# Context keys and values of the cross attention made right behind the last expert tile

## The reference

```python
x = x + _L0_attn_ref(_layernorm(x), W_q, W_kv, W_o)          # layer 0, attention in Fourier space
x = x + _L0_xattn_ref(_layernorm(x), k, skip, ctx, ctx, 8)   # layer 0, long convolution
x = x + _L0_ffn_ref(_layernorm(x), ...)                      # 8 experts, each token goes to 2
x = x + _L1_attn_ref(_layernorm(x), ...)                     # stage 4 of the kernel
x = x + _L1_xattn_ref(_layernorm(x), ctx, wq, bq, wkv, bkv, wp, bp)   # stage 5
x = x + _L1_ffn_ref(_layernorm(x), w_gate, w_up, w_down)     # stage 6
```

```python
q = _qdq(x) @ _qdq(wq).T + bq        # _qdq: rounded to 255 levels of the row's largest magnitude
kv = cond @ wkv.T + bkv              # cond is the context: nothing here depends on x
k, v = jnp.split(kv, 2, axis=-1)
attn = jax.nn.softmax(jnp.einsum('bnhd,bmhd->bhnm', q, k) * scale, axis=-1)
o = jnp.einsum('bhnm,bmhd->bnhd', attn, v).reshape(B, N, C)
out = _qdq(o) @ _qdq(wp).T + bp
```

## Time and profile before

| | |
|---|---|
| median of three runs | 777.13 us (776.04 to 778.58) |
| span of the profiled execution | 774.9 us |
| busy PE / DVE / ACT / POOL | 590.2 / 459.4 / 319.3 / 257.2 us |
| mean granted clock of PE | 0.887 of full speed |

### The profile page before, as it was taken

How to read it: one execution, slowest core, us unless ns; L and a number is a source line. 1 busy time by engine, 2 the same in 40 slices (tenths; PEclk the granted TensorE clock), 3 DMA queues, 4 the chain that set the end, 5 groups by cost and what they waited for, 6 DMA issues and landing times.

```text
span 774.9 us, 12670 instructions
## 1 busy us (share of the span) xinstructions
PE 590.2 (76%) x4241; PEld 425.4 (55%) x4242; DVE 459.4 (59%) x998; ACT 319.3 (41%) x747; POOL 257.2 (33%) x300
## 2 busy tenths in 40 slices
PE   3857896447499999999356989899889677763674
PEld 3446343434288888898223656576575265542332
DVE  3677999672544555455254453535365736767686
ACT  1511200423333333333254654717473535555454
POOL 4930687656000000000366863909423300000000
PEclk9969999555699999999878999999999889895698
DMA  7694202455401101110242000000001300000000
GB/s 273 222 369 154 87 0 66 152 173 207 156 29 54 54 27 54 54 55 19 62 129 65 1 0 2 1 1 0 1 1 47 117 1 3 2 2 1 0 27 27
DMA packets 34251, 52.17 MB, mean 67 GB/s; under 512 B 3097, under 2 KB 24161, under 8 KB 33825
## 3 DMA queue, kind: packets, MB, share of 16 engines
q1 hardware_dynamic: 31680, 43.49, 16.9%
q0 software_dynamic: 2528, 8.13, 2.9%
HBM read 40.60 MB, written 11.01 MB: 67 GB/s over the span
## 4 chain that ended last, share of the span: by engine, by line
PE 52%; DVE 16%; POOL 12%; ACT 11%; issue 4%; DMA 3%; another core or an unknown queue 0%; SPq 0%; ACTq 0%; DVEq 0%
PE bank L1536 16%; PE bank L1549 5%; PE bank L1685 4%; POOL sm L509 3%; POOL rq L502 3%; POOL qs L504 2%; POOL rq L500 2%; PE bank L1415 2%; ACT pT L805 2%; PE bank L1444 2%; PE bank L1446 2%; PE bank L1445 2%; DMA wraw<-in_L_ffn_W 1%; PE bank L1845 1%; PE bank L1946 1%
## 5 line engine op out<-in xcount | busy, mean ns | idle before, releaser
L659 ACT ACTIVATE hf<-bank,be 128x256 f32<-128x256 f32 x120 | 50.4, 471 | 79.4 <-PE bank L1536 73.1
L1536 PE MATMUL bank<-h,wsp 128*128 128x256 f16 x720 | 81.3, 273 | 2.2 <-DVE h L1090 1.5
L490 POOL DMA_INDIRECT yg<-expert_rows,pos x16 | 15.5, 970 | 192.5 <-DMA expert_rows<-yb 188.0
L1536 PEld LDWEIGHTS bank<-h,wsp 128*128 x720 | 69.6, 98 | 12.1 <-issue 3.9
L1088 DVE CAST h<-hf 128x512 f16<-128x512 f32 x60 | 25.6, 427 | 65.8 <-ACT hf L659 64.3
L704 ACT ACTIVATE sm<-sm,nm 128x128 f32<-128x128 f32 x128 | 49.8, 394 | 1.0 <-DVE nm L1201 1.0
L472 POOL TENSOR_TENSOR kvp<-xnT,cxT 128x512 f32<-128x512 f32 x32 | 35.7, 1137 | 42.3 <-ACT xnT L563 32.4
L569 ACT CAST wsp<-wraw 128x2048 f16<-128x2048 f32 x12 | 22.6, 1900 | 63.5 <-DMA wraw<-in_L_ffn_W 63.5
L449 POOL TENSOR_TENSOR wsp<-wraw,wsp 128x512 f16<-128x512 f32 x40 | 45.8, 1178 | 8.7 <-ACT wsp L569 8.4
L1198 DVE SCALAR_TENSOR_TENSOR sm<-bank,const 128x512 f32<-128x512 f32 x32 | 22.1, 691 | 38.5 <-PE bank L1652 38.5
L1536 PE MATMUL bank<-xgT,wsp 128*128 128x256 f16 x360 | 44.2, 282 | 0.1
(11 more groups left out here) (295 smaller groups left out, 1342.7 us busy)
## 6 DMA issues: line engine op xcount, KB each, us to landing
wraw<-in_L_ffn_W SPq DMA_DIRECT2D x16, 512.0 KB
wraw<-in_L_ffn_W SPq DMA_DIRECT2D x8, 1024.0 KB
sorted_rows<-early POOLq DMA_DIRECT2D x2, 1920.0 KB, 16.6
xg<-sorted_rows SPq DMA_DIRECT2D x15, 256.0 KB, 2.8
expert_rows<-yb SPq DMA_DIRECT2D x15, 256.0 KB, 2.2
cxT<-in_ctxT SPq DMA_DIRECT2D x2, 1024.0 KB, 9.1
tap<-in_taps SPq DMA_DIRECT2D x1, 2048.0 KB, 13.9
x<-in_x SPq DMA_DIRECT2D x1, 1024.0 KB, 5.9
```

The source lines that it names most:

```text
L659: last = nc.scalar.activation(hf[:, p, SLOTS * k:SLOTS * k + SLOTS], bank[2 * (layer - 1) + p][:, SLOTS * k:SLOTS * k + SLOTS], ACT.Gelu, ...
L1536: last = nc.tensor.matmul(b[:, SLOTS * (f % 2):SLOTS * (f % 2) + SLOTS], w[a_][:, c, P * f:P * f + P], inp[:, b_, c, :], start=(c == 0 and ...
```

## The change

The products of the context with `wkv` move from stage 5 to the end of the experts, and so does what belongs to them.

- **Inputs.** SP issues `wkvT`, `bv5` and `bk5` before its loop over the expert tiles, then waits for `wab_moved` and issues `cxT` (1 MB). ACT's copy of `wab` into `wqb` (1536 columns) stands for that after the first hidden layer of the first expert tile, no longer after the last tile.
- **Places.** `wkvT` lies beside `wqb` in the place of the raw expert weights; `kx2` and `vpad` lie over the split expert weights; `bv5` and `bk5` lie over `b3` and `wg`.
- **PE** makes the values (16 matmuls) and the keys (8 matmuls) right behind the last expert tile. The values use banks 6, 7, 0, 1 and the keys banks 2, 6, 7, 1, so the keys wait for DVE's reading of the values.
- **DVE** waits for the last expert product, then clears half of `vpad` (2048 elements a partition), sets the ones, makes `bkm` and adds the values' bias.
- **ACT** writes the keys, two products before and two after the first `deviation` of stage 4.
- **Stage 5.** `sdiag` is made on ACT, by 8 instructions of 128 columns, where POOL did it in one; POOL keeps only the clearing of `n4` and the sum with `bp5`, both behind `xi_ready`. The queries go to banks 6, 7, 4, 5. `queries_keys(0)` waits for two of the four `q5T` (semaphore `prep5_act` at 14) and no longer for all four query products; that wait stands in `keys_queries(0)`.

```diff
@@ SP
+            sp.dma_start(wkvT[:], ...).then_inc(sem("context5_loaded"), 16)
+            sp.dma_start(bv5[:], ...).then_inc(sem("context5_loaded"), 16)
+                sp.dma_start(bk5[:], ...).then_inc(sem("context5_loaded"), 16)
+            sp.wait_ge(sem("wab_moved"), 1)
+            sp.dma_start(cxT[:].rearrange("p c t s -> p (c t s)"), a["ctxT"]).then_inc(sem("cxT_loaded"), 16)
             with sp.Fori(0, ET // 2 - 1) as i:
...
@@ POOL
-            pool.wait_ge(sem("x4_added"), NT + 1)
-            nc.gpsimd.memset(vpad[:].rearrange("p t h d -> p (t h d)"), 0.0).then_inc(sem("prep5_pool"), 1)
+            pool.wait_ge(sem("w5_loaded"), 64)
+            pool.wait_ge(sem("xi_ready"), 1)
             nc.gpsimd.memset(n4[:].rearrange("p u n -> p (u n)"), 0.0).then_inc(sem("prep5_pool"), 1)
-            pool.wait_ge(sem("prep5_pool"), 1)
-            nc.gpsimd.memset(vpad[:, :, :, 16:17], 1.0).then_inc(sem("prep5_pool"), 1)
-            pool.wait_ge(sem("scale5_ready"), 1)
-            nc.gpsimd.tensor_tensor(sdiag[:], ..., ALU.mult).then_inc(sem("prep5_pool"), 1)
-            pool.wait_ge(sem("w5_loaded"), 112)
-            pool.wait_ge(sem("xi_ready"), 1)
             nc.gpsimd.tensor_tensor(x[:], x[:], bp5[:].unsqueeze(1).to_broadcast([P, NT, D]), ALU.add).then_inc(sem("prep5_pool"), 1)
@@ ACT
             hidden(1, 0, 0)
+            act.wait_ge(sem("w_split_dve"), 6)
+            nc.scalar.copy(wqb[:, :, 0]..., wab[:]...).then_inc(sem("wab_moved"), 1)
             with act.Fori(0, ET // 2) as i:
...
+            act.wait_ge(sem("bkm_ready"), 1)
+            keys5(0)
+            keys5(1)
             deviation(4, 0, 2)
+            keys5(2)
+            keys5(3)
             xnT_pair(0)
...
+            act.wait_ge(sem("scale5_ready"), 1)
+            for t in range(NT):
+                nc.scalar.activation(sdiag[:, t, :], cst["ident"], ACT.Copy, scale=xsc[:, 1, t:t + 1]).then_inc(sem("sdiag_ready"), 1)
@@ DVE
+            dve.wait_ge(sem("l3_psum"), ET)
+            then(nc.vector.memset(vpad[:, :, :, 16:32], 0.0))
+            nc.vector.memset(vpad[:, :, :, 16:17], 1.0)
+            dve.wait_ge(sem("context5_loaded"), 48)
+            nc.vector.tensor_tensor(bkm[:], ..., ALU.mult).then_inc(sem("bkm_ready"), 1)
+            for k in range(4):
+                dve.wait_ge(sem("prep5_psum"), k + 1)
+                nc.vector.tensor_tensor(vpad[:, 2 * k:2 * k + 2, :, 0:16], bank[VALUE_BANKS[k]]..., ALU.add).then_inc(sem("v5_ready"), 1)
@@ PE
+            pe.wait_ge(sem("context5_loaded"), 48)
+            pe.wait_ge(sem("cxT_loaded"), 32)
+            for k in range(4):
+                values_of(k)
             pe.wait_ge(sem("y_ready"), ET + CREDIT)
+            for k in range(4):
+                c, half = k // 2, k % 2
+                if k:
+                    pe.wait_ge(sem("v5_ready"), (1, 2, 4)[k - 1])
+                for ic in range(DC):
+                    last = nc.tensor.matmul(bank[KEY_BANKS[k]][:], wkvT[:, ic, P * c:P * c + P], ...)
+                last.then_inc(sem("prep5_psum"), 1)
...
             turn_pair(1)
+            pe.wait_ge(sem("prep5_act"), 8)
             queries_low(0, 0)
...
             def queries_keys(p):
                 pe.wait_ge(sem("prep5_act"), 14 if p < 4 else 16)
                 if p == 0:
-                    pe.wait_ge(sem("q5r_ready"), 4)
+                    pe.wait_ge(sem("prep5_act"), 12)
                     pe.wait_ge(sem("v5_ready"), 4)
...
             def keys_queries(p):
                 pe.wait_ge(sem("nT_ready"), p + 1)
+                if p == 0:
+                    pe.wait_ge(sem("q5r_ready"), 4)
```

More of the change, by code:

```diff
@@ L227, in decoder_kernel @@
         wqb = sb("wqb", [P, 3, 2, 8, 64], F32, sq4)
+        wkvT = sb("wkvT", [P, DC, 512], F32, sq4)
         sq4.close()
@@ L268, in decoder_kernel @@
         ewT = sb("ewT", [P, 2, DC, D], BF16, s5)
-        bkm = sb("bkm", [P, DC, 2], F32, s5)
-        kx2 = sb("kx2", [P, DC, NT, 2, P], F32, s5)
-        vpad = sb("vpad", [P, NT, H4, 32], F32, s5)
         sdiag = sb("sdiag", [P, NT, P], F32, s5)
@@ L669, in _ @@
             hidden(1, 0, 0)
+            act.wait_ge(sem("w_split_dve"), 6)
+            nc.scalar.copy(wqb[:, :, 0].rearrange("p c h n -> p c (h n)"), wab[:].rearrange("p c h n -> p c (h n)")).then_inc(sem("wab_moved"), 1)
             with act.Fori(0, ET // 2) as i:
@@ L676, in _ @@
             expert_out(ET // 2, 0)
-            act.wait_ge(sem("w_split_dve"), 6)
-            nc.scalar.copy(wqb[:, :, 0].rearrange("p c h n -> p c (h n)"), wab[:].rearrange("p c h n -> p c (h n)")).then_inc(sem("wab_moved"), 1)
             preload(ACT.Ln)
@@ L685, in xnT_pair, with keys5 @@
                                bank[3 + i][:].rearrange("p (c n) -> p c n", c=DC)).then_inc(sem("xnT_act"), 1)
+            def keys5(k):
+                c, half = k // 2, k % 2
+                act.wait_ge(sem("prep5_psum"), k + 5)
+                for par in range(2):
+                    nc.scalar.activation(kx2[:, c, 4 * half:4 * half + 4, par, :], bank[KEY_BANKS[k]][:].rearrange("p (t s) -> p t s", t=4), ACT.Identity,
+                                         bias=bkm[:, c, par:par + 1], scale=cst["parity"][:, par:par + 1]).then_inc(sem("prep5_act"), 1)
+            act.wait_ge(sem("bkm_ready"), 1)
+            keys5(0)
+            keys5(1)
             deviation(4, 0, 2)
+            keys5(2)
+            keys5(3)
             xnT_pair(0)
@@ L1251, in _ @@
                 dve.wait_ge(sem("prep5_act"), half + 11)
[L1252 to L1253 removed]
+                dve.wait_ge(sem("prep5_psum"), k + 13)
+                nc.vector.tensor_tensor(q5r[:, 2 * k:2 * k + 2, :].rearrange("p t s -> p (t s)"), bank[QUERY_BANKS[k]][:],
                                         sx5[:, 4 * half:4 * half + 4, :].rearrange("p t s -> p (t s)"), ALU.mult).then_inc(sem("q5r_ready"), 1)
[L1255 to L1259 removed]
             def most(p):
@@ L1576, in _, with values_of @@
                     turn_rows(i + 1, u)
-            pe.wait_ge(sem("y_ready"), ET + CREDIT)
+            def values_of(k):
+                for t in range(2 * k, 2 * k + 2):
+                    for ic in range(DC):
+                        last = nc.tensor.matmul(bank[VALUE_BANKS[k]][:, D * (t % 2):D * (t % 2) + D], cxT[:, ic, t, :], wkvT[:, ic, D:2 * D], start=(ic == 0), stop=(ic == DC - 1))
+                last.then_inc(sem("prep5_psum"), 1)
[3 more added lines that the diff above has]
+                values_of(k)
+            pe.wait_ge(sem("y_ready"), ET + CREDIT)
+            for k in range(4):
+                c, half = k // 2, k % 2
+                if k:
+                    pe.wait_ge(sem("v5_ready"), (1, 2, 4)[k - 1])
+                for ic in range(DC):
+                    last = nc.tensor.matmul(bank[KEY_BANKS[k]][:], wkvT[:, ic, P * c:P * c + P],
+                                            cxT[:, ic, 4 * half:4 * half + 4, :].rearrange("p t s -> p (t s)"), start=(ic == 0), stop=(ic == DC - 1))
+                last.then_inc(sem("prep5_psum"), 1)
             pe.wait_ge(sem("w4_loaded"), 48)
@@ L1759, in _ @@
             x_done(pe, 4, NT - 1)
-            pe.wait_ge(sem("w5_loaded"), 112)
-            pe.wait_ge(sem("cxT_loaded"), 32)
-            for c in range(DC):
-                for half in range(2):
-                    for ic in range(DC):
-                        last = nc.tensor.matmul(bank[2 * c + half][:], wkvT[:, ic, P * c:P * c + P],
-                                                cxT[:, ic, 4 * half:4 * half + 4, :].rearrange("p t s -> p (t s)"), start=(ic == 0), stop=(ic == DC - 1))
-                    last.then_inc(sem("prep5_psum"), 1)
+            pe.wait_ge(sem("w5_loaded"), 64)
             pe.wait_ge(sem("prep1_ready"), 6)
@@ L1776, in turn_x @@
                     last.then_inc(sem("xiT_psum"), 1)
-            def values_of(k):
-                for t in range(2 * k, 2 * k + 2):
-                    for ic in range(DC):
-                        last = nc.tensor.matmul(bank[(4, 5, 0, 1)[k]][:, D * (t % 2):D * (t % 2) + D], cxT[:, ic, t, :], wkvT[:, ic, D:2 * D], start=(ic == 0), stop=(ic == DC - 1))
-                last.then_inc(sem("prep5_psum"), 1)
             pe.wait_ge(sem("eqi_ready"), 1)
```

68 lines of the change are left out of this document (28 added, 40 removed).

## The result

| | kernel before | changed kernel |
|---|---|---|
| median of the timed runs, us | 777.33 (773.76 to 780.83, 6 runs) | 770.66 (762.68 to 772.0, 6 runs) |
| span of the profiled execution, us | 774.9 | 770.2 (772.0 in all) |

The ratio of the changed kernel's time to the time before is 0.9897, 95% interval 0.9864 to 0.993: about 8 us faster. The prediction was 767.1 us, with a range from 763.8 to 771.0. The median lies inside the range, 3.6 us above the value. A second series of the same kernel gave 766.59 us (764.9 to 770.25, 6 runs; ratio 0.9888, 0.9859 to 0.9918). The mean of all twelve runs is 768.0. Of the six runs of the version with halves, two (771.55 and 775.66 us, the profiled one) lie over 1.5% above its fastest; its ratio is made from the other four, whose median is 765.98.

The account below looks back on a forecast made before the run. Stage 5's preparation was bound by a DVE-PE chain holding 7.06 us of value matmuls, while PE waited 16.64 us after the experts. -2.4 - 7.9 + 0.3 = -10.0 us: span 764.9, median 767.1, range 763.8 to 771.0.

Parts of the forecast that it names:

- (a): Stage 5's preparation: without POOL's clearing of vpad, DVE's L906 falls from 2.29 to 0.17 us, -2.1 us.
- (b): Stage 5's preparation: without POOL's sdiag, DVE's eight L1235 blocks take 2.24 us and not 3.88, -1.6 us.
- rival C: Stage 5: the two long DVE lines are not POOL's doing, only the values' 7.9 us go: 769.5 us; chance 0.06.
- (c): Stage 5: sdiag costs ACT 2.6 us, its spreading ends 1.4 us after xi; (a) to (c) together -2.4 us.
- (d): Stage 5's preparation: the values leave and nothing of the 7.92 us comes back as a wait, -7.9 us.
- rival A: Stage 5's preparation: PE at full clock there, so L1805 and perhaps first scores run faster: -12.7, 764.4 us; chance 0.15.
- (e): Behind stage 5's first scores ACT is the next to be late, with 0.7 us left: not late.
- (f): Stage 5's first scores: L1827 now follows half-clock matmuls and may slow by 0 to +1.2 us; +0.3 taken.
- Start of the experts: ACT's copy of wab fits into idle time and the third tile's rows land in time: cost 0, at worst +1 us.
- End of the experts: Values and keys fit into PE's 16.64 us wait before the first turn: 0, with ends -0.5 and +2.5 us.
- rival B: Before stage 4, late keys or a falling clock give back +1 to +3.5 us: about 769.5 us; chance 0.22.
- D: Rival: without the values the loop stays at half clock in all seven later blocks, +22 us: 779; chance 0.03.

Follow-up runs that it names:

- the version with halves: Changed kernel, but PE spreads the first four sdiag blocks once ACT has made four, not all eight; median 767.7 us, ratio 0.9859.
- the version with filler: Changed kernel with sdiag spread in halves, plus nine unread 512-column products while PE waits for sdiag; median 765.52 us, ratio 0.986.
- With the values back: Changed kernel with value products and DVE's four additions again between query products and first scores, keys left early; median 777.06 us, ratio 1.0012.
- its version with fillers: Kernel before plus unread products in stage 4's first waits and stage 6's tiles; median 776.56 us, ratio 1.0001.
- warm everywhere: Halves and nine unread products in the preparation, plus unread products in stage 4's first waits and stage 6's tiles, against changed kernel; 762.52 us, ratio 0.9837.
- changed, warm in 4 and 6: Changed kernel plus unread products in stage 4's first waits and stage 6's tiles, none in stage 5's preparation; median 759.62 us, ratio 0.9803.

## Why the prediction was right, and where it was not

**(a), (b): right.** L906 was forecast at 0.17 and took 0.17; the eight blocks at 2.24 took 2.19. Both stalls return when POOL works (2.35 and 3.83 us), so rival C is out.

**(c): right in kind.** `sdiag` took ACT 2.44 us (2.6 forecast, from L840's row), the spreading 3.78 (3.52). It ended 16.2 us after the last sum of stage 4 (614.45 less 598.21), as forecast (612.2 less 595.95). `xi` was ready at 612.94, so the spreading is later by 1.5 us (1.4 forecast). What I did not see is that the turn behind it would run in part at half clock: 1.69 us, where it took 1.07 in the kernel before (as in the version with filler).

**(d): the sum right, by luck; the term for the queries wrong.** The chain of waits of the changed kernel:

```profile
617.43 0.70 DVE xn L1266
618.16 1.53 ACT xnT L795 x2
619.73 1.27 PE bank L1836 x16
```

The query products, which I left at 3.45 us (half clock), ran in 1.90 at full, as rival A had it. And "Nothing of the 7.92 us comes back as a wait" failed: PE waits 1.11 us for `xnT`. These two errors are one. Before, the second `q5T` was ready 3.4 us after the start of the query products (616.47 to 619.9), just as they ended. Now it is ready 3.0 us after it (616.7, with the first record missing from the trace, to 619.7), and in the kernel before's second profile, with full clock, 2.9. So the full clock ends the products 1.5 us sooner and the scores start only 0.4 sooner; the rest is the wait. The way from the end of the spreading to the query products, with the slower turn, took 2.2 and not 1.9 us. -1.5, +1.1 and +0.3 cancel: 21.52 us measured, 21.6 forecast. With the values back, the wait is hidden again, and the step measures 6.7, not 7.9. The forecast's 31.9 before came from a profile with its queries at half clock; against the one with full clock (30.20) the same change wins 8.7.

**(e): right.** ACT was free in time; L802 waited 1.06 us for PE (0.7 forecast).

**(f): the number right, its ground not.** The scores took 1.27 us in the chain, 1.24 before (+0.3 forecast). The products in front of them ran at full clock and not at half, so the case that I priced didn't come.

**Start of the experts: right, no cost.** ACT's copy of `wab` stood at 211.46 for 1.47 us, SP issued `cxT` at 212.96 and the third tile's rows at 213.69, and PE turned them at 222.74 without a wait (222.68 before).

**End of the experts: right to half a us** for every instruction that was placed. The last addition ended at 383.5 (383.6 forecast), the last key product at 389.65 (390.1), the first pair was turned at 392.3 (at most 393), `xnT_pair(0)` started at 393.06 (by 393.6). The remark on the gathers was not put to a test: DVE's memset ended at 378.13, the first gather came at 378.91.

**The clock in stage 4: mis-sized.** The 0 with an upper end of +2.5 "if the clock falls there" was too low. Seven profiles have both products at the end of the experts and no filler in stage 4. Two took 203.2 and 203.3 us, as before; five took 205.9 to 207.3. Their mean is 205.9, +2.5 us (205.7 without the version with halves). The two kernels with only one of the groups there took 203.5 (one profile each), the kernel before 203.3 and 203.45. The records show the way: before, PE stood idle from 375.86 on, its clock was already at half at the first turn, and back at full by 400. Now PE works until 390, the first turn runs at full clock (0.63 us, 1.09 before), and the clock falls behind that:

```profile
402.00:408.00 6.00, 6.00 (x14) 2.67 (x13) 2.21 (x8) 1.89 (x4) 0.92 (x2) 0.55 0.43 126
```

This is the version with halves, PE without a gap and at half clock in the first queries, on which the softmax of the first pair hangs. Four of the five slower executions have the first four records of these queries at 2.08 us, where the kernel before took 1.13; the fifth, the changed kernel's first profile, falls one group of queries later, at 407. The idle stretch in front of the second turn was 1.4 to 2.2 us, not the 3 of the forecast. So rival B was half true: its late keys did not come, its clock did, in five profiles of seven. That the change is the cause is likely and not shown: there are only two profiles of the kernel before as it is, and its version with fillers took 205.55.

**The rest: not given back.** The limit of +1 us on the time from the first scores to the end was broken by the first profile (+3.4) but not by the second (-0.6). Over the nine profiles of the changed kernel and its variants without products in stage 6 the mean is 148.6 us, over two of the kernel before 148.0. The limit was too narrow for a term that moves by 4 us between runs of the same code.

**Rivals A and D.** A had the clock of the queries right and the sum wrong (764.4), because the wait for `xnT` took most of it back. D didn't come. Its figure was wrong as well: 767.1 and 22 make 789, not 779.

**The sum.** By the means of the two profiles of each kernel as it is: preparation -9.6, stage 4 +1.2, rest +0.5, first turn -0.8; together -8.7. With the +2.5 of the seven profiles for stage 4 it would be -7.4. The timed means differ by 8.2 (768.0, twelve runs, against 776.2, 51 runs). The forecast's -10.0 had the preparation nearly right and lacked what the clock takes in stage 4. The first series' median, 770.66, lies outside the forecast's own 765.5 to 768.5; that the stated range holds it is owed to the room left for rival B.

## What to carry to other kernels

Independent products that stand on the path belong into an earlier wait, and the gain can be read from the profile to some tenths; look then for the next operand that the moved work had hidden (here `xnT`, 1.1 us). Filling a long wait of PE can also move where its clock falls (stage 4 took 205.9 to 207.3 us in five of seven executions, 203.3 to 203.45 before), so ask what runs behind the filled wait, and give that a cost above zero. Two terms of a sum can hang on the same clock: faster products show the next operand as late. Where the granted clock differs between executions, one profile can't give a difference of some us: compare stretch by stretch over several. Unread products in PE's short waits before the end won 7 us here in one kernel and nothing in the other, so they have to be measured each time.

## What was not expected of the hardware

- The same kernel's PE is granted full speed or half in the same instructions from one execution to the next: twelve records in 3.05 or 5.05 us in stage 4, the rest of the kernel in 146.41 or 150.47.
- DVE's eight blocks take 3.83 to 3.88 us beside POOL's `sdiag` (1.90 to 2.05 us) and 2.19 alone: 1.6 to 1.7 of POOL's 2 us are lost to DVE. An instruction of 8 elements a partition took 2.29 and 2.35 us, where it takes 0.17, and ended with a memset of POOL that had begun before it.
- With six unread products of 256 columns in each tile, the clock was 1.00 over the last 36 us in one execution (warm everywhere), and in another (changed, warm in 4 and 6) 0.81 over the last 10; without them it was 0.64 over the last 30 us of the changed kernel's first profile.
